# A graph-attention and graph-mixing kernel: work moved between four engines, and an own slot for each stage of each engine

## What is computed

```python
h = jnp.maximum(_layernorm(x, axis=-1), 0.0)
x = x + attention(h, adj)            # 8 heads of 16: softmax(where(adj, q k / 4, -inf)) v, then W_out
h = jnp.maximum(_layernorm(x, axis=-1), 0.0)
z_l, z_g, v = h @ Wl, h @ Wg, h @ Wv
zn = z_l / max(|z_l|, 1e-8);  A_l = zero_diag(max(zn zn^T, 0))      # cosines
A_g = zero_diag(exp(-max(|z_i|^2 + |z_j|^2 - 2 z_i.z_j, 0) / 2))    # distances of z_g
K = 0.9 * rows_to_one(A_l * adj) + 0.1 * rows_to_one(A_g * adj)
x = x + (K @ v) @ Wo
```

## Time and profile before

| | us |
|---|---|
| runs | 990.64, 993.87, 997.05 (median 993.87) |
| profiled execution | 983.95 |
| its span from first to last instruction | 981.9 |
| PE busy in the span | 876.3 (89%) |
| DVE busy | 760.2 (77%) |
| ACT busy | 464.2 (47%) |
| POOL busy | 170.6 (17%) |
| mean granted TensorE clock | 0.989 of full |

### The profile page before, as it was taken

The page is one execution under the profiler, slowest core; times in us unless marked ns, Lnnn a source line. Parts: engine busy times, 40 slices in busy tenths (PEclk is TensorE's granted clock), DMA queues, the critical chain, the costliest instruction groups (busy, mean ns, idle before and its releaser), DMA issues.

```text
span 981.9 us, 15346 instructions
## 1 busy us (share of the span) xinstructions
PE 876.3 (89%) x4991; PEld 496.0 (51%) x5075; DVE 760.2 (77%) x2461; ACT 464.2 (47%) x833; POOL 170.6 (17%) x224
## 2 busy tenths in 40 slices
PE   1479989999999999999999999999899999999987
PEld 1323345646455554645555464555546464655565
DVE  3767778788787878878688887878887887878465
ACT  1015555354545545364554545454454545455531
POOL 5312030121212021121202112120301212010110
PEclk9999989999999999999999999999999999999998
DMA  1331212030212103030211203021120302100000
GB/s 48 107 97 44 77 48 62 20 101 2 87 33 67 53 28 92 3 103 18 73 47 36 85 9 104 10 76 44 50 71 20 101 2 78 32 12 1 12 11 11
DMA packets 65534, 48.46 MB, mean 49 GB/s; under 512 B 10672, under 2 KB 65456, under 8 KB 65456
## 3 DMA queue, kind: packets, MB, share of 16 engines
q1 hardware_dynamic: 65456, 47.48, 15.9%
HBM read 30.28 MB, written 16.78 MB: 48 GB/s over the span
## 4 chain that ended last, share of the span: by engine, by line
PE 63%; DVE 25%; issue 4%; ACT 3%; SPq 2%; DMA 2%; POOL 1%; POOLq 0%; DVEq 0%; ACTq 0%
PE adj L516 11%; PE pv L509 10%; PE turned L497 8%; PE score L486 8%; PE adj L521 8%; PE turned L496 6%; DVE scrap L706 6%; PE work L527 6%; DVE adj_cos L841 3%; PE work L516 3%; DVE bn_sb L684 2%; DVE x_norm L693 2%; SPq L337 2%; PE work L616 1%; PE work L598 1%
## 5 line engine op out<-in xcount | busy, mean ns | idle before, releaser
L870 ACT ACTIVATE probs_t<-turned 128x512 f32<-128x512 f32 x512 | 306.0, 598 | 263.8 <-PE turned L497 251.3
L706 DVE CUSTOM_DVE_ANT_0 scrap<-score,mask_add 128x512 f32<-128x512 f32 x512 | 338.9, 683 | 30.3 <-PE score L486 29.4
L486 PE MATMUL score<-qk_rows 96*128 96x512 bf16 x512 | 202.6, 398 | 9.5 <-DVE neg_max L706 6.1
L497 PE MATMUL turned<-qk_rows 99*128 99x512 bf16 x512 | 195.5, 382 | 7.7 <-DMA qk_rows<-max_rows 2.9
L496 PE MATMUL turned<-bar_t,ident_b 128*128 128x512 bf16 x428 | 164.0, 383 | 0.8 <-DMA qk_rows<-max_rows 0.8
L509 PE MATMUL pv<-probs_t,v_cols 128*32 128x512 f32 x1024 | 137.3, 609 | 0.0
L486 PEld LDWEIGHTS score<-qk_rows 96*128 96x128 bf16 x512 | 50.2, 99 | 110.6 <-DVE neg_max L706 55.2
L497 PEld LDWEIGHTS turned<-qk_rows 99*128 99x128 bf16 x512 | 50.8, 99 | 58.8 <-issue 1.6
L428 POOL TENSOR_SCALAR var_eps<-moments 128x4 f32<-128x4 f32 x16 | 3.8, 237 | 427.6 <-DVE moments L688 427.6
L521 PEld LDWEIGHTS adj<-z,adj_cos 128*128 128x128 f32 x512 | 67.4, 193 | 10.7 <-DVE adj_cos L729 1.3
L521 PE MATMUL adj<-z,adj_cos 128*128 128x130 f32 x512 | 68.9, 278 | 1.5 <-DVE adj_cos L729 0.8
(11 more groups left out here) (107 smaller groups left out, 1102.3 us busy)
## 6 DMA issues: line engine op xcount, KB each, us to landing
qk_rows<-split_dram SPq DMA_DIRECT2D x384, 64.0 KB, 2.3
split_dram<-split SPq DMA_DIRECT2D x32, 384.0 KB, 2.6
...
qk_rows<-max_rows SPq DMA_DIRECT2D x96, 4.0 KB, 1.7
...
```

What stands on the lines that cost most here:

```text
L486: pe.matmul(score_bank[u % 2][:, :], qk_rows[0:ROWS, b % 2, 0, h, t * P:(t + 1) * P], qk_rows[0:ROWS, b % 2, 1, h, :], start=True, stop=Tr ...
L497: pe.matmul(turned_bank[w % 2][:, :], qk_rows[0:ROWS + 3, b % 2, 1, h, j * P:(j + 1) * P], qk_rows[0:ROWS + 3, b % 2, 0, h, :], start=Fals ...
L706: dve.tensor_tensor_reduce(scrap[:, u % 2, :], score_bank[u % 2][:, :], mask_add[:, u % T, :], -1.0, 3.0e38, ALU.add, ALU.min, neg_max[:, ...
L870: act.activation(probs_t[:, k % 4, w % HG, :], turned_bank[w % 2][:, :], ACT.Exp, scale=SCALE).then_inc(probs_ready.sem, 1)
```

## The change

1. A table with an entry for each engine's part of a stage. Before, an engine's part stood in the slot of the stage; now, for instance, the z product, its copy and its square sums have slots of their own, and nearly all stages move. On SyncE the order in a round becomes: output (2), `col_store` (5), `col_load` (8), row stores (10), first maxima (14), next x (18), row loads (20 and 22), second maxima (31).
2. Both normalisations' multiply goes from VectorE to ScalarE, as relu(x * rstd + shift), with the relu that stood behind the turn. GpSimd computes the shift, -mean * rstd, with two more small instructions for each normalisation.
3. The square sums go from VectorE to ScalarE: eight 128x128 Square activations with an accumulator in each round, two behind each copy of z.
4. The turned row of `rbf_bias` is no longer made on TensorE and ScalarE: a DMA stores the 512 numbers to DRAM one by one, and another loads them spread over 128 partitions.
5. Of each four turned tiles the first gets no mask matmul. GpSimd multiplies the bits of its exponentials, as integers, with 0 or 1 (`keep_t`, 128x512 int32), in place, before the `attend` that reads them.
6. The waits for a free PSUM bank are derived from the table for `adj_bank` too.

The diff, cut to what the prediction speaks of:

```diff
--- before.py
+++ after.py
+MASK_BY_PE = (1, 2, 3)
...
 AT = {
-    "ln_moments": (-32,), "ln_scale": (-30,), "hT": (-29,), "hT_split": (-28,), "ln_rstd": (-27,),
-    "q": (-26,), "k": (-24,), "qk_store": (-22,), "rows0": (-18,), "x_biased": (-16,), "x_next": (-14,),
-    "v": (-12,), "rows1": (-11,),
-    "max_split": (16, 32), "max_turn": (17, 33),
-    "pv": (28, 32, 36, 40, 44, 48, 52, 56), "pv_copy": (41, 57), "y": (44, 59), "yT": (60,), "attn": (62,),
-    "ln2_moments": (63,), "ln2_rstd": (63,), "ln2_scale": (66,), "h2T": (68,), "z": (70, 71, 72, 73),
-    "z_sums": (74,), "zgT": (74,), "zgT_read": (75,), "z_norms": (76,), "col": (78,), "zlT": (79,),
-    "rbf": (81, 83, 89, 93), "rbf_exp": (82, 84, 90, 93), "rbf_mask": (84, 86, 92, 95),
-    "cos": (82, 89, 92, 94), "mix_cos": (95, 96, 100, 102), "mix_rbf": (96, 98, 100, 102), "store": (103,),
+
+    "hT": (-26,), "q": (-24,), "k": (-22,), "v": (-15,), "max_turn": (16, 32),
+    "pv": (28, 32, 36, 40, 44, 48, 52, 56), "y": (54, 59), "yT": (61,), "attn": (62,), "h2T": (67,),
+    "z": (69, 70, 72, 73), "zgT": (77,), "zlT": (79,), "rbf": (79, 83, 85, 87), "cos": (81, 83, 86, 89),
+    "mix_cos": (92, 94, 96, 98), "mix_rbf": (94, 95, 96, 98),
+
+    "ln_scale": (-28,), "hT_copy": (-26,), "q_hi": (-24,), "k_hi": (-22,), "max_copy": (16, 32),
+    "pv_copy": (40, 57), "yT_copy": (60,), "ln2_scale": (64,), "h2T_hi": (67,), "z_copy": (69, 70, 72, 74),
+    "z_sums": (71, 73, 74, 75), "zgT_hi": (77,), "zlT_hi": (78,), "rbf_exp": (82, 83, 85, 88),
+
+    "ln_moments": (-35,), "hT_split": (-26,), "q_rest": (-24,), "k_rest": (-21,), "v_add": (-12,),
+    "max_split": (15, 32), "y_scale": (55, 60), "x1": (62,), "ln2_moments": (62,), "h2T_lo": (67,),
+    "zgT_lo": (77,), "zlT_lo": (79,), "rbf_read": (81, 83, 85, 87), "cos_read": (81, 83, 87, 90),
+    "rbf_mask": (84, 85, 90, 93), "out": (94, 96, 98, 99),
+
+    "ln_rstd": (-31,), "q_split": (-25,), "k_split": (-18,), "x_biased": (-15,), "ln2_rstd": (61,),
+    "z_norms": (75,),
+
+    "qk_store": (-22,), "rows": (-12, -10), "x_next": (-14,), "max_load": (14, 31), "col_store": (69,),
+    "col_load": (72,), "store": (98,),
 }
-FIRST, LAST = -32, 104
+FIRST = min(min(at) for at in AT.values())
+LAST = max(max(at) for at in AT.values()) + 1
...
+    by_pe = [w for w in range(SLOTS) if w % HG in MASK_BY_PE]
+    by_pool = [w for w in range(SLOTS) if w % HG not in MASK_BY_PE]
...
-        WORK_TURNS = sorted(
...
+        for t in range(T):
+            BANK_READ["z", t] = (z_ready, t + 1)
+            BANK_READ["cos", t] = (cos_ready, t + 1)
+            BANK_READ["rbf", t] = (rbf_arg_ready, t + 1)
+            BANK_READ["mix_cos", t] = (out_ready, t + 1)
+
+        def bank_turns(*stages):
+
+            turns = sorted((AT[name][nth] + SLOTS * b, order, name, nth, b)
+                           for b in range(B) for order, (name, nth) in enumerate(stages))
+            return [turn[2:] for turn in turns]
+
+        work_turns = bank_turns(
+            ("max_turn", 0), ("max_turn", 1), ("hT", 0), ("q", 0), ("k", 0), ("v", 0), ("y", 0), ("y", 1),
+            ("yT", 0), ("attn", 0), ("h2T", 0), ("zgT", 0), ("zlT", 0))
+        adj_turns = [
+            bank_turns(*[("cos", m) for m in range(T)], ("mix_cos", 0), ("mix_cos", 2), ("z", 0), ("z", 2)),
+            bank_turns(*[("rbf", m) for m in range(T)], ("mix_cos", 1), ("mix_cos", 3), ("z", 1), ("z", 3)),
+        ]
+
+        def bank_free(engine, turns, batch, name, nth=0):
+
+            place = turns.index((name, nth, batch))
             if place:
-                _, _, name, nth, batch = WORK_TURNS[place - 1]
-                sig, count = WORK_DONE[name, nth]
+                name, nth, batch = turns[place - 1]
...
             for s in slots:
-                if hit := due(s, "max_turn"):
+                if hit := due(s, "max_load"):
...
-                if hit := due(s, "rows0"):
-                    load_rows(hit[0], 0)
-                if hit := due(s, "rows1"):
-                    load_rows(hit[0], 1)
+                if hit := due(s, "rows"):
+                    load_rows(*hit)
                 if (hit := due(s, "x_next")) and hit[0] + 1 < B:
                     b, _ = hit
                     reached(sp, ln_done, b)
                     reached(sp, x_resid_ready, b)
                     load_x(b + 1)
+                if hit := due(s, "col_store"):
+                    b, _ = hit
+                    reached(sp, rbf_bias_ready, b)
+                    reached(sp, col_ready, b - 1)
+                    sp.dma_start(col_dram.rearrange("(t p) -> p t", p=P), rbf_bias[:, :],
+                                 allow_slow_non_contiguous=True).then_inc(col_stored.sem, 16)
+                if hit := due(s, "col_load"):
+                    b, _ = hit
+                    reached(sp, col_stored, b)
+                    reached(sp, rbf_arg_ready, b - 1)
+                    sp.dma_start(col_term[:, :], col_dram.partition_broadcast(P)).then_inc(col_ready.sem, 16)
...
+                if hit := tile_due(s, LAG + 1):
+                    b, w = hit
+                    if w in by_pool:
+                        if (b, w) == (0, by_pool[0]):
+                            pool.wait_ge(s_keep.sem, 1)
+                        reached(pool, probs_ready, b, w + 1)
+                        tile = probs_t[:, w // HG % 4, w % HG, :].bitcast(I32)
+                        pool.tensor_tensor(tile, tile, keep_t[:, w // HG % T, :],
+                                           ALU.mult).then_inc(probs_masked.sem, 1)
...
+                    pool.tensor_scalar(neg_mean[:, :], moments[:, :, 0], -1.0, None,
+                                       ALU.mult).then_inc(ln_neg.sem, 1)
                     reached(pool, ln_var, b)
                     pool.tensor_tensor(rstd[:, :], var_eps[:, :], minus_half[:, :],
                                        ALU.pow).then_inc(ln_rstd.sem, 1)
-                for which, name in enumerate(("q", "k")):
+                    reached(pool, ln_neg, b)
+                    reached(pool, ln_rstd, b)
+                    pool.tensor_tensor(ln_shift[:, :], neg_mean[:, :], rstd[:, :],
+                                       ALU.mult).then_inc(ln_shifted.sem, 1)
...
-                pe.matmul(turned_bank[w % 2][:, :], ident_b[:, :], bar_t[:, j, :], start=True, stop=False)
+                if w in by_pe:
+                    pe.matmul(turned_bank[w % 2][:, :], ident_b[:, :], bar_t[:, j, :], start=True, stop=False)
                 pe.matmul(turned_bank[w % 2][:, :], qk_rows[0:ROWS + 3, b % 2, 1, h, j * P:(j + 1) * P],
-                          qk_rows[0:ROWS + 3, b % 2, 0, h, :], start=False,
+                          qk_rows[0:ROWS + 3, b % 2, 0, h, :], start=w not in by_pe,
                           stop=True).then_inc(turned_filled.sem, 1)
...
-                reached(pe, probs_ready, b, ends)
+                reached(pe, probs_masked, b, sum(w < ends for w in by_pool))
+                if by_pe:
+                    reached(pe, probs_ready, b, 1 + max(w for w in by_pe if w < ends))
...
                 if hit := due(s, "mix_cos"):
                     b, n = hit
                     if n == 0:
                         reached(pe, cos_ready, b)
-                    elif n == 1:
-                        reached(pe, rbf_arg_ready, b)
-                    else:
-                        reached(pe, out_ready, b, n - 1)
+                    bank_free(pe, adj_turns[n % 2], b, "mix_cos", n)
...
-                if hit := due(s, "col"):
-                    b, _ = hit
-                    reached(pe, rbf_bias_ready, b)
-                    work_bank_free(pe, b, "col")
-                    turn_tiles(lambda t: rbf_bias[:, t:t + 1].broadcast_to([P, P]), col_filled)
...
-                    last = dve.tensor_copy(mask_t[:, m, :], src[:, :])
-                last.then_inc(s_mask_copied.sem, 1)
-                dve.wait_ge(s_mask_copied.sem, 1)
+                    dve.tensor_copy(mask_t[:, m, :], src[:, :])
+                    last = dve.tensor_copy(keep_t[:, m, :], src[:, :])
...
-            def layer_norm_scale(dst, src, mv, inv_std, done):
-                for t in range(T):
-                    last = dve.tensor_scalar(dst[:, t, :], src(t), mv[:, t, 0:1], inv_std[:, t:t + 1],
-                                             ALU.subtract, ALU.mult)
-                last.then_inc(done.sem, 1)
...
-                if hit := due(s, "z_sums"):
-                    b, _ = hit
-                    reached(dve, z_ready, b)
-                    reached(dve, rbf_bias_ready, b - 1)
-                    for t in range(T):
-                        for a in range(2):
-                            part = z[:, t, a * D:(a + 1) * D]
-                            last = dve.tensor_tensor_reduce(z_square[:, t, a * D:(a + 1) * D], part, part,
-                                                            1.0, 0.0, ALU.mult, ALU.add,
```

(29 more changed lines are left out.)

137 lines of the change are left out of this document (72 added, 65 removed).

## The result

The changed kernel takes 1032.72 us (median of 4 runs, 1029.43 to 1033.97) against 994.5 before: 1.038 times as long (95% interval 1.034 to 1.043). The forecast was 938.5 with a range of 905 to 978. The kernel is slower, and outside the range.

The account below looks back on a forecast made before the run. TensorE was taken to bound the round (busy 52.9 of 56.4 us), VectorE's bursts costing the rest. Savings in fill, eleven rounds (29.7) and end sum to 54.8: 983.95 becomes 929.2, as run median 938.5; range 905 to 978.

Parts of the forecast that it names:

- the column's term: Column by DMA: store 3.6 us, load 3.16, against 7.2 until VectorE's first rbf read; 0.3 lost a round, up to 1.2.
- signs of being wrong: Rounds above 56, second table load, `col_store` beyond 5, rbf masks well over 0.69, masks above 2.5, or GpSimd's norms late.
- rival E: Squares on ScalarE need another function table: eight loads, 10 us a round, about 1090 us; 0.08 together with a slow trip.
- slow trip: The column's store and load make the kernel slower only from 12 us; 0.08 together with rival E.
- The slack: Time from `rbf_bias` to VectorE's first rbf read: 7.2 us, against 7.5 for the column to arrive by DMA.
- ScalarE's burst: Slots 4 to 13: ScalarE has 16.8 us of work against TensorE's 13.9; TensorE waits 3.0 us a round in all.
- the walk: TensorE's and ScalarE's queues followed slot by slot with the prices; 938.5 us predicted, its own range 920 to 955, chance 0.50.
- The masks: Eight of 32 mask matmuls leave TensorE, 1.8 us less a round; on GpSimd 1.28 each, hidden.
- The fill: Windows before the steady rounds: x and maxima go ahead of row loads; 5.8, 5, 4 and 3.5 us saved.
- The end: Last window, 146.05 us: one ordinary round saves 2.8, the last round 4 by masks, column turns and later squares.
- Rival B: No burst: relus and squares near lower bounds, bank waits free of stalls; 51.5 us a round, 907 us; chance 0.17.
- The shared path: GpSimd holds VectorE's SBUF-to-SBUF instructions (hT's cast and split, rbf masks): 1.4 us a round, at worst 993 us; chance 0.10.

Follow-up runs that it names:

- l512: The changed kernel with a load of 512 single numbers from a constant DRAM row in place of the column's store, distance part left out; 910.19 us, 0.923 of before.
- s128: The changed kernel storing 128 single numbers side by side instead of 512, the load reading a constant row, distance part left out; 985.97 us, 0.997 of before.
- c1: The changed kernel with the column's store as 128 runs of 16 bytes from a constant tile, distance part left out; 911.39 us, 0.918 of before.
- q1: v1 with the eight square sums of a round back on VectorE; 954.56 us, 0.959 of before.
- v0: v1 with all 32 masks on TensorE, none on GpSimd; 943.18 us, 0.947 of before.
- v1: The changed kernel, complete, with the column stored as 128 runs of 16 bytes and VectorE reading it with a step; 920.02 us, 0.925 of before.
- a1: The changed kernel with the column turned on TensorE and copied by ScalarE again, no DMA trip; 917.68 us, 0.924 of before.

## Why the prediction was wrong, point by point

**The step that failed** is the column's term, "512 single ones lie between 2.4 and, if each adds what those 128 add, 1.7 + 4 x 0.7 = 4.5: I take 3.6", and with it "The load, 256 KB, is as x: 3.16". They were 9.0 and 5.0, 14.0 for 6.8 together, and a round lost 7.2 by it where the forecast allowed 0.3. The bound of 4.5 rested on `bias_q` in the earlier trace rows, which is a load. As loads, 512 single numbers do stay within the bounds: 2.1 in l512. It was the direction and the neighbourhood in memory that the row did not have (as a store, the same 512 took 1.9 when they lay apart, 9.0 side by side): no row of before writes single numbers to DRAM. Two of the signs of being wrong that the prediction names came with it, rounds above 56 (58.9) and `col_store` beyond 5 (9.0). I called the extrapolated value an upper bound although the operation was of another kind, and the range inherited it. The case was named, "The column's trip would do it only from 12 us", in the rival E with a slow trip at 0.08 together. It was worked out well and weighed badly: s128, with 11.6, lands at 0.997 of before, and at 14.0 the gain is lost and 38 us more.

**The slack was about right.** "That is 7.5 from `rbf_bias` to the first rbf read, and VectorE is there 7.2 later": with a quick store the read starts 8.3 later, without a wait. The forecast expected the trip nearly to vanish in it, and up to 6.3 it does. Not counted was the second price of a wait, the low clock behind it: of the 79.3 us that the change's eleven rounds lose against c1's, 24.9 are TensorE's longer busy time. So the wait cost about one and a half times what TensorE stood still for it (79.3 for 54.4 there, 49.6 for 30.5 in s128).

For the store the Trainium skill, page DMA: Bandwidth & Descriptors, Specifications, has a rule that I did not weigh: the full rate needs transfers of 512 bytes or more, and below that the DMA reads, modifies and writes. It gives no price in time. The runs do not bear its limit out as a measure of the time: runs of 16 bytes took 1.4 us, and single numbers 1.9 when they lay apart. That neighbouring writes of 4 bytes wait for each other's read and write would fit both; that is argued, and no run here looks inside a DMA engine.

**ScalarE's burst was over-priced**: 3.0 forecast. In c1, which has the forecast's matmuls, TensorE is busy 50.0 of a round's 51.7 and waits 1.7: 0.4 for the split of z_g and 1.3 for the split of z_l on VectorE. It waits for no exponential and not for q's remainder, for which the walk had some 2. The forecast's 50.4 of work was too much by 0.4 at least, since busy time is an upper bound. The walk spaced exponentials 0.64 apart. The timeline of ScalarE in the changed kernel (start us, us) shows what it does in a burst:

```profile
296.28 0.58 ACT L967 CAST h2T_parts<-work 128x512 fp32r<-128x512 f32 x1
296.88 0.60 ACT L903 ACTIVATE probs_t<-turned 128x512 f32<-128x512 f32 x1
297.37 1.64 ACT L912 ACTIVATE x_norm<-x_sb,ln_shift,rstd 128x128 f32<-128x128 f32 x4
298.91 0.58 ACT L903 ACTIVATE probs_t<-turned 128x512 f32<-128x512 f32 x1
```

What stands behind an exponential starts 0.49 later, though the exponential's record is 0.60 long, and four relus take 1.54 to the next start, not 2.0. The rows of before give busy times of single instructions, and where ScalarE has work waiting, consecutive ones overlap by 0.1. The Trainium skill, page ScalarE: Activation LUTs, What ACT_TABLE_LOAD costs, has this: "Back-to-back ACTIVATEs overlap by ≈ 93 ns". The trace agrees (0.60 less 0.49), and the prediction's estimate by that page, 1.5 for a set of relus, is what the timeline shows, where the walk took 2.0. The rule that relu and multiplications belong on VectorE (the Trainium skill, the same page, Rules for kernel authors) would have had it wrong here for the squares: on ScalarE they are worth 34 us (q1), for on VectorE they stand ahead of maxima for which TensorE waits. Whether it is wrong for the multiply of the normalisations too, no run shows.

**The other steps**, by window; c1 stands for the change with a trip that is in time:

| window | before | forecast | c1 | after |
|---|---|---|---|---|
| to the first turned score | 68.5 | 62.7 | 64.3 | 64.0 |
| second | 39.1 | 34.1 | 35.9 | 36.3 |
| third | 49.5 | 45.5 | 45.7 | 54.8 |
| fourth | 57.9 | 54.4 | 51.7 | 58.2 |
| eleven rounds | 620.9 | 591.2 | 568.3 | 647.6 |
| the end | 146.1 | 139.2 | 144.0 | 170.4 |

- The masks: 1.28 each and hidden, 1.8 us a round as forecast (v0 against v1). Right.
- The fill: right within 2 us. The chain of before has the row loads, the load of x (3.16) and the rows of the maxima (1.70) behind them on its way to the first turned score; the changed kernel's has neither x nor the maxima's rows, as was named. The lower clock there was not forecast, and what it cost is not separated.
- The end: -2 in c1 for -6.8. With no next graph's work around it the last second block is a bare chain, in which squares and relus on ScalarE lie open; it also runs at a lower clock (0.95 over the window in c1, and 0.87 and 0.80 in the two halves of its last 40.9 us, where before has 0.91). In a1's last 40.7 us the squares between the copies of z hold four places of the chain (0.69, 0.59, 0.77 and 0.39), 2.4 us.
- The table load: there is one, as before. Rival E's first half did not come. Rival B, the short burst and waits free of stalls, was forecast at 907; it is what c1 (911) shows, and what the change would have been with a trip of up to 6.3 us.
- The shared path: real, and priced well, at 1.4 us a round on VectorE for 1.8 in c1. But its victims are mostly not those of size that were named, hT's cast and split: beside the rbf masks it is the short splits of the maxima. VectorE had time to spare for it elsewhere in the round, but not there: the split of z_l, for which TensorE waits 1.3, stands right behind them. What that wait would be without them no run shows. The masks are not to blame for it, as v0 to v1 has TensorE's full 1.8.
- Not tested alone: the multiply on ScalarE, the new slots and the derived waits for banks. Masks (23 us) and squares (34 us), priced in v1's table, are most of the 72 us by which c1's span is shorter than before's; how the rest divides stays open.

So the loss of 49 us in span divides: with a quick trip (c1) the span is 909.9, 72 below before; the slow trip adds 121, of which 79 in the eleven rounds, 26 in the end, where the last graphs' trips have little beside them, and 16 in the third and fourth window.
